# Start addresses of the attention product's operand tiles, and the spacing of the moving rows

## The reference, cut to what matters

```python
u = h @ h.T / sqrt(384);  p = softmax(u);  delta = p * adjacency
attn = delta / (delta.sum(axis=2, keepdims=True) + 1e-10)
h_left, h_self, h_right = (h @ W.T + b for (W, b) in ((W_left, b_left), (W_self, b_self), (W_right, b_right)))
ctx = where(j > i, attn, 0) @ h_left + diagonal(attn)[:, None] * h_self + where(j < i, attn, 0) @ h_right
gnn = relu(layernorm(ctx, 1e-12) * gamma + beta)
out = layernorm(x + gnn, 1e-5)
```

## Time and profile before

| | before |
|---|---|
| median of 3 runs | 464.03 us (463.55 to 464.73) |
| the profiled execution, its own time | 464.28 us |
| its span, first to last instruction | 462.6 us |
| TensorE busy, share of the span | 450.8 us, 97% |
| VectorE, ScalarE, GpSimd busy | 83%, 69%, 44% |
| mean granted TensorE clock | 0.994 |

### The profile page before, as it was taken

One profiled execution on the slowest core, in us unless ns is written; L12 is line 12 of the kernel. 1 busy time (PEld: TensorE's weight loads), 2 busy tenths in 40 slices (PEclk: granted clock), 3 DMA queues, 4 the chain that ended last, 5 costly groups with the idle time before them and its releaser, 6 DMA issues.

```text
span 462.6 us, 9443 instructions
## 1 busy us (share of the span) xinstructions
PE 450.8 (97%) x2639; PEld 448.5 (97%) x2639; DVE 384.6 (83%) x1118; ACT 320.9 (69%) x709; POOL 204.9 (44%) x290
## 2 busy tenths in 40 slices
PE   8999999999999999999999999999999999999982
PEld 8999999999999999999999999999999999999981
DVE  5777988878888888988887988887888887898875
ACT  6756677677678677677777667776767767766742
POOL 0144345554345553345554444554334555334521
PEclk9999999999999999999999999999999999999997
DMA  8765455665555665545566455566546556554221
GB/s 253 225 205 178 128 173 188 191 194 184 160 174 181 187 215 185 156 161 182 177 215 193 144 179 173 190 198 193 159 162 187 188 188 193 182 161 142 81 74 69
DMA packets 84134, 80.59 MB, mean 174 GB/s; under 512 B 7058, under 2 KB 76436, under 8 KB 84116
## 3 DMA queue, kind: packets, MB, share of 16 engines
q1 hardware_dynamic: 84112, 80.38, 55.1%
q10 hardware_dynamic: 4, 0.00, 0.0%
HBM read 52.04 MB, written 28.31 MB: 174 GB/s over the span
## 4 chain that ended last, share of the span: by engine, by line
PE 93%; DVE 2%; ACT 1%; DMA 1%; issue 1%; POOL 0%; SPq 0%; POOLq 0%; DVEq 0%
PE ps_proj L478 62%; PE ps_ctx L514 21%; PE ps_scores L470 3%; PE ps_scores L464 2%; PE ps_scores L466 2%; PE ps_scores L416 2%; DMA dt_raw<-dt_dram 1%; PE ps_proj L446 0%; DMA dt_dram<-turned 0%; PE ps_proj L500 0%; POOL rstd L1079 0%; ACT proj_hi L599 0%; ACT normed L625 0%; SPq L315 0%; DVE proj_lo L800 0%
## 5 line engine op out<-in xcount | busy, mean ns | idle before, releaser
L478 PE MATMUL ps_proj<-w_hi,xt_split 128*128 128x384 f32 x1152 | 304.7, 336 | 1.1 <-ACT ps_proj L595 1.1
L478 PEld LDWEIGHTS ps_proj<-w_hi,xt_split 128*128 128x128 f32 x1152 | 209.1, 188 | 1.6 <-ACT ps_proj L595 1.4
L478 PE MATMUL ps_proj<-w_lo,xt_split 128*128 128x384 f32 x576 | 193.5, 336 | 0.0
L1079 POOL TENSOR_TENSOR rstd<-var_eps,minus_half 128x4 f32<-128x4 f32 x32 | 36.4, 1138 | 194.6 <-DVE var_eps L834 187.8
L478 PEld LDWEIGHTS ps_proj<-w_lo,xt_split 128*128 128x128 f32 x576 | 108.3, 188 | 0.0
L595 ACT ACTIVATE ps_proj<-bias 128x386 f32<-128x386 f32 (+1 forms) x188 | 90.4, 494 | 1.8 <-DVE proj_lo L800 0.8
L1085 POOL TENSOR_TENSOR scaled<-normed,gamma_sb 128x384 f32<-128x384 f32 x60 | 61.0, 1016 | 30.6 <-ACT normed L625 30.6
L619 ACT ACTIVATE ps_ctx<-ps_proj,diag 128x386 f32<-128x386 f32 x64 | 35.6, 557 | 52.4 <-PE ps_proj L478 50.9
L599 ACT ACTIVATE proj_hi<-ps_proj 128x384 fp32r<-128x384 f32 x128 | 63.4, 497 | 9.2 <-PE ps_proj L478 8.6
L800 DVE TENSOR_TENSOR proj_lo<-ps_proj,proj_hi 128x384 fp32r<-128x384 f32 x128 | 67.3, 544 | 1.6 <-ACT proj_hi L599 1.6
L1089 POOL TENSOR_TENSOR shifted<-scaled,beta_sb 128x384 f32<-128x384 f32 x60 | 61.0, 1016 | 2.4
(11 more groups left out here) (87 smaller groups left out, 633.8 us busy)
## 6 DMA issues: line engine op xcount, KB each, us to landing
x_sb<-in_x SPq DMA_DIRECT2D x32, 384.0 KB, 4.4
xt_sb<-in_x_t SPq DMA_DIRECT2D x31, 384.0 KB, 3.9
out_dram<-out_sb SPq DMA_DIRECT2D x31, 384.0 KB, 2.8
adj_sb<-in_adj SPq DMA_DIRECT2D x32, 256.0 KB, 4.4
dt_dram<-turned SPq DMA_DIRECT2D x31, 256.0 KB, 2.0
dt_raw<-dt_dram SPq DMA_DIRECT2D x124, 64.0 KB, 2.0
cross_dram<-cross_turned SPq DMA_DIRECT2D x29, 256.0 KB, 2.0
cross_raw<-cross_dram SPq DMA_DIRECT2D x116, 64.0 KB, 2.0
```

What stands on the lines that cost most here:

```text
L478: mm = nc.tensor.matmul(ps_proj[bank(at, g)][:, 0:H], stationary, moving[w][:, c, :], start=(clear and i == 0), stop=True, skip_group_chec ...
L1079: nc.gpsimd.tensor_tensor(rstd[at.slot(2)][:], var_eps[:], minus_half[:], ALU.pow).then_inc(rstd_ready, 1)
```

## The change

Two small unused tiles are declared, of 64 and of 32 bytes in a partition, and the rows of `proj_hi` and `proj_lo` are made 416 elements (1664 bytes, 13 times 128) long instead of 386. The starts modulo 128 bytes become: `dt_full`, `dt_left`, `dt_right` at 32; every row of `proj_hi` and of `proj_lo` at 64. The 30 added elements of a row are never written or read: `attend` takes `0:HE`, the same 386 columns. Each engine's instructions, their order, sizes and waits are the same. Tiles declared later (the statistics, `normed`, `scaled`, `shifted`, the two bias rows) move along: `normed`, `scaled` and `shifted` from 32 to 64 modulo 128.

```diff
@@ -93,6 +93,7 @@
     BANK = 512
     ONE = H
     HE = H + 2
+    ROW = 416
@@ -149,12 +150,16 @@
         cross_raw = sb("cross_raw", [P, Q, T, T * R])
 
+        sb("dt_place", [P, 16])
         dt_full = sb("dt_full", [P, 2, T * T, P], F32R)
         dt_left = sb("dt_left", [P, 2, T, P], F32R)
         dt_right = sb("dt_right", [P, 2, T, P], F32R)
 
-        proj_hi = sb("proj_hi", [P, NSPLIT, HE], F32R)
-        proj_lo = sb("proj_lo", [P, NSPLIT, HE], F32R)
+        sb("proj_place", [P, 8])
+        proj_hi = sb("proj_hi", [P, NSPLIT, ROW], F32R)
+        proj_lo = sb("proj_lo", [P, NSPLIT, ROW], F32R)
@@ -509,7 +514,7 @@
-                    m_hi, m_lo = proj_hi[:, g, :], proj_lo[:, g, :]
+                    m_hi, m_lo = proj_hi[:, g, 0:HE], proj_lo[:, g, 0:HE]
```

## The result

The changed kernel takes 465.0 us (median of 22 runs, 464.28 to 466.09), the kernel before 464.31 us (22 runs, 463.31 to 466.71): ratio 1.0018, 95% interval 1.001 to 1.0025. The change makes the kernel slower by 0.2%; the forecast was 0.2% faster, and its range ended at 464.8 us. The profiled execution has a span of 463.5 us against 462.6.

What follows compares the result with a forecast made beforehand. TensorE was taken to bound the kernel; the attention rows' gain of 0.99 us, other terms at zero, took the runs' median of 464.03 us to 463.04, rounded to 463.1 us (0.2% faster), range 462.0 to 464.8 us.

Steps and rivals of the forecast that it cites:

- The bound and the cover: TensorE, busy 97%, bounds the kernel; in 31 of 32 batches attention matmul time is wholly on the path.
- the 18: A batch's attention matmuls (L514), first start to next projection: 3.167 us before, forecast 3.135 us after.
- 3.18 or more (the new pair costs): Sign of being wrong: attention matmuls of a batch taking this many us would mean the new operand places cost.
- the value for the rows: Attention matmuls with moved rows and `proj` tiles: 174.2 ns each, gaining 0.032 us a batch, 0.99 us over 31.
- the price of two columns: Attention matmul columns beyond 384: 0.8 to 0.9 ns, from 256- and 384-column pitches, 0.43 ns a column.
- like row: `proj_lo` row 0, second matmul of each attention, at 0 modulo 64, 386 columns: 170 ns from rounded starts.
- just the pair that a projection has: Moving row at 64 and stationary tile a multiple of 128 from `xt_split`: claimed to match projections, supporting 174.2 ns.
- The sixes: Attention starts grouped by six: those with no 16-byte-aligned row slowest, 177.8 ns a matmul against 174.4 in the middle.
- The bounds: Limits for the attention pitch: 173.3 ns, gaining 1.5 us, to L470's 176.7 ns, losing 0.4 us.
- The collision of the new places: Rival: attention operands at 32 and 64 cost L470's 176.7 ns, 0.4 us slower, 464.4 us; chance 0.07.
- The tail of the row: Rival: each new attention row pays for a 25th 64-byte piece, pitch 180 ns, 2.3 us slower, 466.3 us; chance 0.05.
- The count of 16-byte lines: Attention rows of 1544 bytes touch 97 lines at either offset, so the change gives nothing: 464.0 us.

Runs made afterwards that it cites:

- e11: Kernel before with 382 instead of 384 columns in its projection matmuls, no tile moved; 465.78 us.
- e15: Changed kernel with rows 2048 bytes apart at 192 and delta's tiles at 288 modulo 512, as the projections' operands lie; 466.93 us.
- e7: Changed kernel with 400 instead of 386 columns in the attention product; 470.58 us.
- e3: Changed kernel with rows 2048 instead of 1664 bytes apart, so all start at 64 modulo 512; 463.70 us.
- e1: Kernel before with 384 instead of 386 columns in the attention product, row sum left out; 462.49 us.
- e5: Kernel before with only delta's three tiles moved, to 32 modulo 128; 464.88 us.
- e6: Changed kernel with delta's tiles back at 96, so only the projections' rows are moved; 464.69 us.
- e2: Changed kernel with 384 instead of 386 columns in the attention product, row sum left out; 462.12 us.
- e9: Changed kernel with 384 attention columns and the row sum taken by a VectorE reduction; 478.14 us, ratio 1.0307.
- e10: Kernel before, tiles unmoved, with 384 attention columns and the row sum taken by a VectorE reduction; 478.62 us, ratio 1.0315.
- e16: Kernel before with 370 instead of 384 columns in its projection matmuls, no tile moved; 461.78 us.
- e4: Changed kernel with 388 instead of 386 columns in the attention product, the two added ones zeros; 468.17 us.
- e13: Changed kernel with 384 attention columns and the row sum taken by two ScalarE copies with an accumulator; 462.40 us, ratio 0.9965.

## Why the prediction was wrong

- **The bound and the cover were right.** TensorE has no new wait, the writes of the rows cost nothing, and what the attention matmuls lost came through whole: 31 times 33 ns, 1.0 us in the span. The prediction's own sign of being wrong, the 18 at "3.18 or more (the new pair costs)", is what came: 3.197.
- **The failed step is the value for the rows:** "I take the value of the like row, 174.2 ns, for all of them". It rested on three readings. First, the price of two columns, 0.83 ns, came from the difference of the 256- and 384-column pitches; both are whole multiples of 16 columns. e11, e15 and e7 show that between such lengths the pitch does not follow the columns: at the projections' places 382 settle at what 384 cost, and 386 at 180.0 ns, near what 400 cost in e7. Second, `proj_lo` row 0 as the "like row": one pitch of a single matmul. It was read rightly (174.1 ns over 28 batches), but the same matmul, its row still at 0 modulo 64, has 180.0 ns in the changed kernel. e3 shows pitches of 171.6 to 180.0 ns at one and the same pair of places, so a single pitch prices nothing. Third, "just the pair that a projection has": e15 built that pair in full, and had the dearest steady pitch of all 386-column streams.
- **The sixes** (off 16 bytes, slower) were a real row, but not a price per address. With 384 columns at the old places (e1) the groups of three still differ, 514 ns for g = 2 and 526 for g = 1, but the two make 1040 together, twice the 520 of the even pitch. Uneven rows shift time between neighbours. Only what does not come back is lost, and that needed the whole sum.
- **The bounds** were too narrow: 176.7 ns as the upper one, where the changed kernel has 177.6. Nor was 176.7 the price of a place: it is the mean of 174, 176 and 180 ns, right behind matmuls of another length. In time the miss of the range is small and partly the yardstick's: the kernel before had 464.03 us when the forecast was made and 464.31 in the later runs. Against it the change cost 0.7 us, where the range allowed 0.8; 465.0 us is 0.2 above it. The direction and the 18 are wrong by either count.
- **The collision of the new places**, a rival given 0.07 (464.4 us), came nearest in time and had the form right: e5 and e6 show that the pair counts. Its price was too low, and it did not tie it to the length, without which (e2) the new places cost nothing.
- **The tail of the row**, a rival given 0.05, had the sign right and named the right step, 16 columns, with 180 ns. The objection to it (the old rows end inside a piece too) was sound for the size and wrong for the conclusion: a partial piece costs part of a step or all of it, by how the places and the matmuls before fall. At the changed kernel's places it was 177.6.
- **The rules of the Trainium skill.** From the independent ports that the Trainium skill ("TensorE: Matmul & The Clock Gate", part 2, step 1) gives the weight load and the moving stream I had drawn that the place of delta's tiles has no price. e5, which moves only these, has 27 ns a batch more; the measurement decides. The count of 16-byte lines from the Trainium skill ("SBUF — State Buffer", section on the DMA port swizzle) gave no change for the rows, and e6 has 23 ns more.

Shown: length, the pair of places, and the matmuls ahead each change the pitch with the others held. The traces show one more regularity. In the kernel before, the changed one and fourteen of the sixteen experiments (all but e9 and e10, where TensorE waits in the batches), the steady distance of batches is a whole number of 6.667 ns, the time by which 16 columns lengthen a pitch (180.0 - 173.3): 13.7733 us before are 2066 of them, 13.8067 us 2071, e15's 13.8333 us 2075, e11's 13.8267 us 2074. So do the patterns: six matmuls of e3 take 159, seven of e16 180, two of e4's projections 53. Each comes out to a hundredth of a step, though with 386 columns in 18 matmuls the columns of a batch add up to no whole number of sixteens. So a batch gains or loses whole steps and not single columns.

Not shown is the mechanism. That the stream of rows and the loads of the next tile meet in steps of 16 columns, and keep their phase only when each matmul is a whole number of steps long, fits the uneven pitches at 370, 386 and 388 columns. It does not fit three rows of the table: 382's calm 173.3 ns, the last six matmuls of e7 with their 400 columns, and the projections of e4 and e7, which have 384 and still take half a step more each. No run tells either whether the steps belong to the reads of rows, to the loads or to the writes into the bank. Why the old places are the cheapest found for 386 columns stays open; nothing in the runs makes it more than luck.

## What to carry to other kernels

When TensorE is never idle, count what a matmul's last columns cost: here a column of ones and one of padding beyond 384 cost 47 ns a batch at the better places, and taking them off, with the row sum moved to an engine's proven idle time, gained 0.35% (0.19% with the tiles where they were). Don't price an address or a column by one matmul: the same new places gave 10 ns a batch at 384 columns and cost 33 at 386, and 400 columns, a whole number of 64-byte steps too, were uneven there and slowed the projections behind. Compare whole batches. Before adding work to an engine look at what waits for it in turn: 0.67 us on VectorE at 83% cost 3%, and 1.3 us on ScalarE, in a named wait, cost nothing.

## What was not expected of the hardware

- A matmul's pitch depends on matmuls that ended before. After 388 or 400 columns in 18 attention matmuls, the 45 projections behind them ran at a mean of 176.6 to 176.7 ns instead of 173.4, with no wait and with the granted clock at 1.00.
- 386 columns can cost 6.7 ns more than 384, all of what 16 columns cost (e15), and 382, once settled, nothing less (e11).
- In a steady state the distance of batches is a whole number of 6.667 ns in every kernel here but e9 and e10, also where 18 of its matmuls have 386 columns.
- Work of other engines does not show in the pitches: with 1.3 us more a batch on ScalarE (e13 against e2) the 18 take 3.120 us in both, and with 0.67 us more on VectorE (e9) 3.121.
